# Experts computed for chosen token-expert pairs in 23 static tiles, with the routing moved into self-attention

## Chip, cores and metric

One core of a Trainium2 chip (trn2). The time is the device time of one launch in microseconds; of the kernel before three runs were taken (1611.67, 1611.69 and 1613.4, median 1611.69). Profiles are of one execution.

## What is computed

Sixteen sequences of 64 tokens (1024 rows of 512 numbers) pass one layer: cross-attention over 1601 context rows each, causal self-attention, and a mixture of experts. All in float32. The last part, which the change is about:

```python
scores = jnp.einsum('bsd,ed->bse', x, w_gate_router)          # 8 experts
topk_scores, topk_idx = jax.lax.top_k(scores, 2)
topk_probs = jax.nn.softmax(topk_scores, axis=-1)
weights = jnp.sum(topk_probs[..., None] * jax.nn.one_hot(topk_idx, E), axis=-2)
gate = jnp.einsum('bsd,efd->bsef', x, w_gate_proj)             # f = 192
up = jnp.einsum('bsd,efd->bsef', x, w_up_proj)
out = jnp.einsum('bsef,edf,bse->bsd', silu(gate) * up, w_down_proj, weights)
```

Here x is the layer-normalised input, and the result is added to the input. Of the 1024 x 8 (token, expert) pairs, 2048 have a weight that is not zero.

## The kernel before, in words

Everything is written by hand: each engine has its own instruction list in a block per stage, and they meet at semaphores. The stages are prepare, cross_attention (to about 1190 us), self_attention (L1303, to 1371) and experts (L1716). A block ends when all engines are through.

**Precision.** Where a product is made of two float32r halves, split_product (L93) issues three matmuls for each block of 128 rows of the contraction: high by high, high by low, low by high. The halves come from a copy with a cast to float32r (high) and a subtraction (low). transposes (L78) turns blocks of 128x128 by a matmul with the identity.

**self_attention.** Four rounds of two chunks of 128 tokens (i = 0..3, u = 0, 1), three of them in a loop on each engine, each with: queries, keys and values (L1603, L89), scores (L1628), softmax on VectorE (L1503 to L1510), exp on ScalarE (L1415), transposed probabilities, the weighted sum (L1654), normalisation, the transposed output, the output product (L89); between these stand the pieces of the next round's cross-attention output product (L1582) and its normalisation (L1466 to L1487). stats2 (L1536) takes statistics of the finished x. Beside it SP loads the weights of the first two experts into expert_raw in three transfers, and POOL computes their high and low halves (L1371, L1373).

**experts.** First the routing for all 8 chunks of 128 tokens: normalise (L1839), transpose, copy to moe_xT (L1799), split (L1801, L1843), product with the router's 8 columns (L89, eight matmuls of 128x8 a chunk in float32), then on VectorE scores, the two largest, their indices, softmax of two and one row of 8 weights per token (L1860 to L1877). After that a loop over four pairs of experts, two of them in its body, with 8 chunks each. A chunk has gate and up for both experts of the pair, 384 columns each (24 matmuls), silu on ScalarE (L1811), the product with up and the weight on VectorE (L1892), three transposes, the halves (L1816, L1901), the down product of 512 columns (9 matmuls) and the addition into x_sb (L1906). TensorE's order is gate_up(t), transposes of t-1, down2(t-2). Beside it SP loads the next pair's weights, VectorE casts their high halves (L1883, 128x1536 each) and POOL subtracts for the low ones (L1785). At the end SP stores the 8 chunks of x (L1776).

## Time and profile before

| | us |
|---|---|
| median of 3 runs | 1611.69 |
| the profiled execution's own time | 1612.94 |
| its span, first to last instruction | 1611.1 |
| TensorE busy (matmul) | 1535.0, 95% of the span |
| weight loads of TensorE | 1299.7, 81% |
| VectorE busy | 848.6, 53% |
| ScalarE busy | 741.3, 46% |
| POOL busy | 464.7, 29% |
| cross-attention ends | about 1190 |
| self-attention ends | about 1371 |
| first matmul of the experts (L100) | 1394.1 |
| last matmul of the experts | 1607.6 |

How to read it: L100 is the line of the matmul in split_product, whoever calls it; the tiles tell the stage. Matmuls overlap in the pipeline, so one of 384 columns is shown with 335 ns while the next starts 172 ns later; weight loads (PEld) have their own row. Idle time is put before an instruction in brackets, with what ended it. The DMA share is of 16 engines.

### The profile page before, as it was taken

The page shows a single profiled execution, that of the slowest core. Times are in us where ns is not written, and L with a number is a line of the kernel's source. Part 1 is how long each engine was busy: PE and PEld are TensorE (multiplying, and loading weights), DVE is VectorE, ACT ScalarE, POOL GpSimd, SP SyncE. Part 2 cuts the span into 40 slices and gives each one's busy share as a digit, 9 for nine tenths or more (in the row PEclk, how much of TensorE's full clock was granted, in tenths as well). Part 3 has the DMA queues.
Part 4 walks back from the last instruction along what each step waited for, and adds up shares of the span by engine and source line. Part 5 has one row for each costly group of instructions (what it writes and reads, how often), then busy time and mean ns, then how long its engine had stood idle before and what let it go on. Part 6 is the DMA issues. An engine that isn't in the chain of part 4 may idle for free. (4 is left out here: it accounts for less than half of the span.)

```text
span 1611.1 us, 41874 instructions
## 1 busy us (share of the span) xinstructions
PE 1535.0 (95%) x16226; PEld 1299.7 (81%) x16226; DVE 848.6 (53%) x1793; ACT 741.3 (46%) x1515; POOL 464.7 (29%) x492
## 2 busy tenths in 40 slices
PE   5789999999999999999999999999977998899999
PEld 2378888888888888888888888888856666899998
DVE  6756555555655555555565555556535554433333
ACT  2246555555655555555555555555532232311111
POOL 3233333333333333333333333333330000022102
PEclk9989999999999999999999999999998999699999
DMA  6030011000110100001000110000020000121011
GB/s 233 17 94 26 21 29 32 18 25 28 32 28 15 32 28 28 18 29 28 28 20 27 28 32 15 28 28 16 3 60 1 0 0 1 60 59 60 20 38 52
DMA packets 35920, 53.81 MB, mean 33 GB/s; under 512 B 7091, under 2 KB 15670, under 8 KB 35766
## 3 DMA queue, kind: packets, MB, share of 16 engines
q1 hardware_dynamic: 35332, 51.44, 10.5%
q8 instruction: 126, 2.06, 0.5%
q14 instruction: 28, 0.23, 0.0%
q10 hardware_dynamic: 434, 0.08, 0.0%
HBM read 48.89 MB, written 2.62 MB: 32 GB/s over the span
## 5 line engine op out<-in xcount | busy, mean ns | idle before, releaser
L1044 POOL TENSOR_TENSOR ksq<-kc 128x512 f32<-128x512 f32 x200 | 208.1, 1041 | 431.7 <-DVE kc L1089 429.8
L1089 DVE TENSOR_TENSOR kc<-psum,bk_sb 128x512 f32<-128x512 f32 x200 | 138.2, 691 | 239.7 <-PE psum L100 239.6
L954 ACT COPY v_sb<-psum 128x512 f32<-128x512 f32 x192 | 112.7, 587 | 282.3 <-PE psum L100 282.3
L968 ACT ACTIVATE probs<-psum 128x1024 f32<-128x1024 f32 x208 | 202.8, 1023 | 81.7 <-PE psum L1211 81.6
L1211 PE MATMUL psum<-qbd,k 64*128 64x128 f32 x3328 | 216.0, 279 | 4.4 <-issue 4.4
L1037 POOL TENSOR_TENSOR y_lo<-y_sb,y_hi 128x256 fp32r<-128x256 f32 x190 | 139.3, 733 | 231.5 <-ACT y_hi L927 231.4
L1211 PEld LDWEIGHTS psum<-qbd,k 64*128 64x128 f32 x3328 | 195.0, 188 | 11.2 <-issue 7.2
L1228 PEld LDWEIGHTS psum<-v_sb,probs 128*64 128x64 f32 x6144 | 186.9, 138 | 17.6 <-issue 17.5
L1228 PE MATMUL psum<-v_sb,probs 128*64 128x33 f32 x6144 | 197.6, 224 | 0.0
L1095 DVE TENSOR_REDUCE kss<-ksq 128x16 f32<-128x512 f32 x200 | 136.4, 682 | 111.3 <-POOL ksq L1044 111.3
L100 PE MATMUL psum<-wk_hi,y_hi 128*128 128x512 f32 x400 | 176.8, 442 | 11.1 <-issue 9.0
L100 PE MATMUL psum<-wv_hi,y_hi 128*128 128x512 f32 x400 | 158.8, 397 | 0.2 <-ACT v_sb L954 0.2
L100 PE MATMUL psum<-wk_hi,y_lo 128*128 128x512 f32 x400 | 158.0, 395 | 0.0
L100 PE MATMUL psum<-wk_lo,y_hi 128*128 128x512 f32 x400 | 157.4, 393 | 0.0
L100 PE MATMUL psum<-wv_hi,y_lo 128*128 128x512 f32 x400 | 157.3, 393 | 0.0
L100 PE MATMUL psum<-wv_lo,y_hi 128*128 128x512 f32 x400 | 157.2, 393 | 0.0
L940 ACT ACTIVATE k<-psum,cols_sb 128x512 f32<-128x512 f32 x192 | 150.6, 785 | 9.2 <-PE psum L81 8.7
L1104 DVE SCALAR_TENSOR_TENSOR kn<-kc,kr 128x512 f32<-128x512 f32 x200 | 141.4, 707 | 7.3 <-DVE kr L117 0.4
L81 PEld LDWEIGHTS psum<-ident_sb,kn 128*128 128x128 f32 x800 | 99.3, 140 | 27.8 <-issue 1.7
L81 PE MATMUL psum<-ident_sb,kn 128*128 128x128 f32 x800 | 120.1, 273 | 1.3 <-ACT k L940 1.3
L115 DVE SCALAR_TENSOR_TENSOR ktmp<-ktmp,kseed 128x16 f32<-128x16 f32 x200 | 116.5, 583 | 6.8
L1785 POOL TENSOR_TENSOR wg_lo<-expert_raw,wg_hi 128x1536 fp32r<-128x1536 f32 x4 | 14.0, 3490 | 309.6 <-DVE wg_hi L1883 309.6
(223 smaller groups left out, 2311.1 us busy)
## 6 DMA issues: line engine op xcount, KB each, us to landing
y_sb<-in_y SPq DMA_DIRECT2D x48, 512.0 KB, 3.7
expert_raw<-in_wg SPq DMA_DIRECT2D x5, 768.0 KB, 5.1
expert_raw<-in_wu SPq DMA_DIRECT2D x5, 768.0 KB, 4.6
expert_raw<-in_wd SPq DMA_DIRECT2D x5, 768.0 KB, 4.6
out_dram<-x_sb SPq DMA_DIRECT2D x8, 256.0 KB, 2.0
x_sb<-in_x SPq DMA_DIRECT2D x1, 1536.0 KB, 10.2
wq<-in_wq SPq DMA_DIRECT2D x4, 256.0 KB, 5.1
xa_wo<-in_wo SPq DMA_DIRECT2D x1, 1024.0 KB, 12.2
```

The costliest lines, as they stand in the source:

```text
L81: last = pe.transpose(bank[:, k * P:(k + 1) * P], src[:, k * P:(k + 1) * P], ident)
L100: last = pe.matmul(bank, lhs, rhs, start=(n == 0), stop=(n == len(todo) - 1))
L115: nc.vector.scalar_tensor_tensor(out=tmp, in0=tmp, scalar=-0.5, in1=seed, op0=ALU.mult, op1=ALU.mult).then_inc(second, 1)
L940: last = nc.scalar.activation(k32[:, buf(n)], bank, ACT.Identity, scale=g.cols[:, 2:3], bias=g.cols[:, 3:4])
L968: nc.scalar.activation(probs[:, buf(u), :], psum[:, bank:bank + 2, :].rearrange("p a n -> p (a n)"), ACT.Exp, scale=SCALE).then_inc(s["ex" ...
L1037: nc.gpsimd.tensor_tensor(g.y_lo[:, buf(n)], src, g.y_hi[:, buf(n)].bitcast(F32), ALU.subtract).then_inc(s["ylo"], 1)
L1044: nc.gpsimd.tensor_tensor(sq[:, buf(n)], kc[:, buf(n)], kc[:, buf(n)], ALU.mult).then_inc(s["ksq"], 1)
L1089: nc.vector.tensor_tensor(kc[:, buf(n)], psum[:, K_BANK, :], g.bk[:], ALU.add).then_inc(s["kb"], 1)
L1095: nc.vector.tensor_reduce(ss[:, buf(n)], head_view(sq[:, buf(n)]), AX_X, ALU.add).then_inc(s["krd"], 1)
L1104: nc.vector.scalar_tensor_tensor(out=head_view(kn[:, buf(n)]), in0=head_view(kc[:, buf(n)]), scalar=HD ** 0.5, in1=spread(kr[:, buf(n)], H ...
L1211: last = pe.matmul(out[n][a], k32[rows, k_buf(u), n, :], g.qbd[rows, n, :], start=not guarded, stop=True, skip_group_check=True)
L1228: last = pe.matmul(psum[j * SQ:(j + 1) * SQ, V_BANK if n else O_BANK, p * VW1:(p + 1) * VW1], probs[:, buf(u), place(h) * SQ:(place(h) + 1 ...
```

## The change

**Layout.** A row of x in SBUF grows from 512 to 520 numbers: behind the 512 stand the token's number (TOK), the number plus 2048 (TOK_S), the difference of its two weights (GAIN), the smaller weight (WEIGHT), the first expert (FIRST), the higher expert's number (HIGH), 1/sigma (RSTD) and -mean/sigma (SHIFT). A DRAM tensor "slots" has a region of 1024 such rows for each expert and a ninth one. Blank rows, with token numbers in a spare part of the output, are written over all of it in cross_attention: nine DRAM-to-DRAM writes of 1024 rows (2.1 MB each) on SP's queue. The output tensor grows to 3712 rows, of which the first 1024 count.

**Routing.** Rounds i-1 = 0..2 are routed within self_attention's round i, and round 3 in the experts' block. TensorE transposes x as it is (not normalised), multiplies by the router's columns (the mean's part is subtracted by the column sums, route_columns), and counts for each token how many before it chose the same expert (route_ranks: four matmuls of up to 16 columns with a triangular and a ones matrix). VectorE takes statistics, logits, the two largest, indices, weights and each row's place; nearly every step waits for the one before (link: a semaphore per instruction). POOL then writes the 128 rows of each chunk to two places in slots: four indirect DMAs of 128 rows a round. self_attention's loop is unrolled. POOL no longer splits weights there; SP loads two experts' weights (1 MB each) in place of one pair's.

**Tables.** After the last round VectorE computes from the counts for each of 23 tiles its expert, its first row in slots, and where its weights lie (27 small operations). 23 = 16 + 7 is the most that 2048 pairs can fill with tiles of 128 rows of one expert; the number of tiles is the same whatever the routing.

**Tiles.** For each tile SP loads 128 rows (5 buffers), ScalarE normalises them, TensorE transposes them (4), ScalarE and VectorE make halves, TensorE multiplies with gate and up of one expert (12 matmuls of 384 columns, 192 for gate and 192 for up), silu of 192 columns, VectorE's product in three pieces, two transposes, halves, down (6 matmuls of 512), ScalarE multiplies by the weight. POOL stores the rows of y at the token's row of the output where this expert is the token's lower one, adds the layer's input rows to y, and adds the sum by an accumulating indirect DMA where it is the higher one; the other case of each goes to spare rows. A store waits until the store of the tile before has landed. All weights, high and low, stay in SBUF; experts 0 and 1 and the third block of the down weights are split before the first tile, experts 2 to 7 after tiles 0, 1, 2, 4, 5 and 6 (AFTER), the high half on ScalarE, the low one on VectorE, 2048 columns each. TensorE reads three numbers per tile into registers (steer) and addresses its weights by them.

The diff, cut to its core (lines taken out are those of the old experts and of the splits in self_attention):

```diff
+                def blanks(e, n):
+                    sp.dma_start(io["slots"][bass.ds(e * REGION, n * 2 * P), :].rearrange("(a p) c -> a p c", a=n),
+                                 io["blank"][bass.ds(e, 1)].to_broadcast([n, 2 * P, ROW])).then_inc(s["blank"], 16)
+                blanks(E_, E_ // 2)
...
+                    blanks(i, REGION // P // 2)
...
+def route_scatter(nc, io, g, pool, i):
+    r = g.route
+    pool.wait_ge(r.s["place"], i + 1)
+    for u in range(2):
+        for n in range(PICK):
+            nc.gpsimd.indirect_dma_start(
+                io["slots"][:, :], bass.IndirectOffsetOnAxis(ap=r.target[:, i, n, u:u + 1], axis=0),
+                g.x[:, i * 2 + u, :], None).then_inc(r.s["slots"], 16)
...
+    for u in range(2):
+        last = nc.vector.max_index(out=r.idx[:, i, u, :], in_max=r.top[:, i, u, :], in_values=r.logits[:, i, u, :])
+    r.link(dve, nc.vector.tensor_tensor(r.gap[:, i], r.top[:, i, :, 1], r.top[:, i, :, 0], ALU.subtract))
+    nc.vector.tensor_tensor(r.gap_n[:, i], r.gap[:, i], g.x[:, i * 2:i * 2 + 2, RSTD], ALU.mult).then_inc(r.s["gap"], 1)
+    r.link(dve, nc.vector.tensor_copy(r.chosen[:, i], r.idx[:, i, :, 0:PICK]))
+    for n in range(PICK):
...
                 def steps(i, more):
                     qkv(i, 0)
+                    if i:
+                        pe.wait_ge(s["x2"], done(i - 1, 1))
+                        pe.wait_ge(s["xe"], done(i, 1))
+                        route_turn(g, pe, i - 1, 0, psum[:, TR, :])
                     qkv(i, 1)
+                    if i:
+                        pe.wait_ge(r.s["xe"], i * 2 - 1)
+                        route_turn(g, pe, i - 1, 1, psum[:, TR, :])
                     scores(i, 0)
+                    if i:
+                        route_product(g, pe, psum, i - 1, 0)
+                        route_product(g, pe, psum, i - 1, 1)
                     if more:
                         out_product(i + 1, 0, 0)
                     scores(i, 1)
                     if more:
...
+                def rows_in(j):
+                    first = table(sp, "first", j, 0, SLOT_ROWS - P)
+                    if j >= XB:
+                        sp.wait_ge(s["total"], j - XB + 1)
+                    sp.dma_start(rows[:, j % XB, :], io["slots"][bass.ds(first, P), :]).then_inc(s[f"rows{j % XB}"], 16)
+                sp.wait_ge(s["low0"], 1)
+                sp.dma_start(raws[0].rearrange("p (n d) -> p n d", d=D), io["wd_rest"]).then_inc(s["raw0"], 16)
+                sp.wait_ge(s["tables"], 1)
+                sp.wait_ge(r.s["slots"], 16 * ROUNDS * 2 * PICK)
+                for j in range(XB):
+                    rows_in(j)
+                for e in range(2, 5):
+                    load(e)
+                for j in range(XB, TILES):
+                    rows_in(j)
+                    if j in LOADS:
+                        load(LOADS[j])
+                for n in range(2):
+                    sp.wait_ge(s[f"first{n}"], 16 * ((TILES + 1 - n) // 2))
+                    sp.wait_ge(s[f"second{n}"], 16 * ((TILES + 1 - n) // 2))
...
+            @blk.gpsimd
+                pool.wait_ge(s["whi"], 1)
+                nc.gpsimd.tensor_tensor(block(0, 1), raws[0], block(0, 0).bitcast(F32), ALU.subtract).then_inc(s["low0"], 1)
+                route_scatter(nc, io, g, pool, last)
+                for j in range(TILES):
+                    n = j % 2
+                    pool.wait_ge(s["y"], j + 1)
+                    if j:
+                        pool.wait_ge(s[f"first{1 - n}"], 16 * ((j + 1) // 2))
+                    nc.gpsimd.indirect_dma_start(
+                        io["out"][:, :], bass.IndirectOffsetOnAxis(ap=at_first[:, j:j + 1], axis=0),
+                        y[:, n, :], None).then_inc(s[f"first{n}"], 16)
+                    if j >= 2:
+                        pool.wait_ge(s[f"second{n}"], 16 * (j // 2))
+                    nc.gpsimd.tensor_tensor(total[n], y[:, n, :], rows[:, j % XB, 0:D], ALU.add).then_inc(s["total"], 1)
+                    pool.wait_ge(s["total"], j + 1)
+                    nc.gpsimd.indirect_dma_start(
+                        io["out"][:, :], bass.IndirectOffsetOnAxis(ap=at_second[:, j:j + 1], axis=0),
+                        total[n], None, compute_op=ALU.add).then_inc(s[f"second{n}"], 16)
...
+                def x_norm(j):
+                    act.wait_ge(s[f"rows{j % XB}"], 16 * (j // XB + 1))
+                    if j >= 2:
+                        act.wait_ge(s["tr"], j - 1)
+                    row = rows[:, j % XB, :]
+                    nc.scalar.activation(xn[:, j % 2], row[:, 0:D], ACT.Identity, bias=row[:, SHIFT:SHIFT + 1],
+                                         scale=row[:, RSTD:RSTD + 1]).then_inc(s["xn"], 1)
...
+                def scale(j):
+                    act.wait_ge(s["dn"], j + 1)
+                    act.wait_ge(s["weight"], j + 1)
+                    if j >= 2:
+                        act.wait_ge(s[f"first{j % 2}"], 16 * (j // 2))
+                        act.wait_ge(s["total"], j - 1)
+                    nc.scalar.activation(y[:, j % 2], psum[:, DN + j % 2, :], ACT.Identity, scale=weight[:, j:j + 1]).then_inc(s["y"], 1)
...
+                route_evac(nc, g, act, last, 0, psum[:, TR, :])
+                route_evac(nc, g, act, last, 1, psum[:, TR + 1, :])
+                route_seed(nc, g, act, last)
+                high(0)
+                route_exp(nc, g, act, last)
+                high(1)
+                act.wait_ge(s["raw0"], 16)
+                nc.scalar.copy(rest[:, 0].rearrange("p n d -> p (n d)"), raws[0]).then_inc(s["rest_hi"], 1)
+                x_norm(0)
+                x_norm(1)
+                x_high(0)
+                x_high(1)
+                for j in range(TILES + 1):
+                    if 0 < j and j + 1 < TILES:
+                        x_high(j + 1)
+                    if j < TILES:
+                        silu(j)
+                    if j:
+                        scale(j - 1)
+                    if j < TILES:
+                        h_high(j)
+                    if j + 2 < TILES:
+                        x_norm(j + 2)
+                    for e in range(2, E_):
+                        if AFTER[e] == j:
+                            high(e)
...
+                route_stats(nc, g, last, 1)
+                route_norm(nc, g, dve, last)
+                route_logits(nc, g, dve, psum, last)
+                route_top(nc, g, dve, last)
+                route_rows(nc, g, dve, last)
+                route_place(nc, g, dve, psum, last)
+                route_tables(nc, g, dve)
+                dve.sem_inc(s["tables"], 1)
+                dve.wait_ge(s["low0"], 1)
+                low(1)
+                dve.wait_ge(s["rest_hi"], 1)
+                nc.vector.tensor_tensor(rest[:, 1].rearrange("p n d -> p (n d)"), raws[0],
+                                        rest[:, 0].rearrange("p n d -> p (n d)").bitcast(F32), ALU.subtract).then_inc(s["rest_lo"], 1)
+                x_low(0)
+                x_low(1)
+                for j in range(TILES):
+                    weights(j)
+                    hidden(j)
+                    if 0 < j and j + 1 < TILES:
+                        x_low(j + 1)
+                    h_low(j)
+                    for e in range(2, E_):
+                        if AFTER[e] == j:
+                            low(e)
...
+                def gate_up(j, base, need):
+                    pe.wait_ge(s["xhi"], j + 1)
+                    pe.wait_ge(s["xlo"], j + 1)
+                    pe.wait_ge(s["wlo"], need)
+                    if j >= 2:
+                        pe.wait_ge(s["hid"], j - 1)
+                    terms = [(x_hi[:, j % 2, k, :], x_lo[:, j % 2, k, :], w[:, bass.ds(base + k * 2 * F, 2 * F)],
+                              w[:, bass.ds(base + (WHALF + k * 2 * F), 2 * F)]) for k in range(KD)]
+                    split_product(pe, psum[:, GU + j % 2, 0:2 * F], terms).then_inc(s["gu"], 1)
...
+                def steer(j):
+                    return (table(pe, "block", j, 0, (E_ - 1) * WBLOCK), table(pe, "at", j, 0, (E_ // 2 - 1) * D),
+                            table(pe, "need", j, 1, E_))
...
+                held = [steer(0)]
+                turn(0)
+                for j in range(TILES + 1):
+                    if j + 1 < TILES:
+                        held.append(steer(j + 1))
+                        turn(j + 1)
+                    if j < TILES:
+                        gate_up(j, held[j][0], held[j][2])
+                    if j:
+                        down(j - 1, held[j - 1][0], held[j - 1][1])
+                    if j < TILES:
+                        turn_hidden(j)
...
```

## Rows read from the trace of the kernel before

**Rows 1.** The page, part 2: the clock granted to TensorE, in 40 slices of 40.3 us, in tenths.

```profile
PEclk9989999999999999999999999999998999699999
```

**Rows 2.** Busy time by stretch (us, count), then PEclk, DMA share, GB/s.

```profile
1217.60:1371.00 153.40, 141.25 (x1067) 102.19 (x1065) 75.85 (x152) 45.32 (x104) 0.00 (x0) 0.99 0.00 1
1371.00:1394.10 23.10, 19.96 (x96) 19.69 (x96) 10.42 (x27) 11.32 (x19) 0.00 (x0) 0.51 0.32 104
1394.10:1398.50 4.40, 4.40 (x15) 4.40 (x15) 3.52 (x33) 1.49 (x2) 0.00 (x0) 0.50 0.00 0
1398.50:1609.00 210.50, 209.49 (x1140) 194.87 (x1139) 71.96 (x143) 28.05 (x64) 41.84 (x12) 1.00 0.14 43
...
1347.00:1362.00 15.00, 9.53 (x121) 7.12 (x122) 9.32 (x14) 5.70 (x11) 0.00 (x0) 1.00 0.00 1
```

**Rows 3.** Timeline (start, us) of one chunk's weight loads in the expert stage.

```profile
1402.51 0.19 PEld L100 LDWEIGHTS psum<-wu_hi,moe_xhi 128*128 128x128 f32 x1
...
1404.59 0.42 PEld L81 LDWEIGHTS psum<-ident_sb,moe_h 128*128 128x128 f32 x3
...
1404.99 0.19 PEld L100 LDWEIGHTS psum<-wg_hi,moe_xhi 128*128 128x128 f32 x1
...
1409.48 0.19 PEld L100 LDWEIGHTS psum<-wd_hi,moe_hhi 128*128 128x128 f32 x1
...
1411.46 0.19 PEld L100 LDWEIGHTS psum<-wg_hi,moe_xhi 128*128 128x128 f32 x1
```

**Rows 4.** Timeline and page: single durations (page: xcount, busy, mean ns, idle).

```profile
L1044 POOL TENSOR_TENSOR ksq<-kc 128x512 f32<-128x512 f32 x200 | 208.1, 1041 | 431.7 <-DVE kc L1089 429.8
...
L940 ACT ACTIVATE k<-psum,cols_sb 128x512 f32<-128x512 f32 x192 | 150.6, 785 | 9.2 <-PE psum L81 8.7
...
1331.12 0.38 ACT L1396 COPY sa_xT<-psum 128x256 f32<-128x256 f32 x1
...
1350.17 1.22 DVE L1508 TENSOR_REDUCE sa_mx<-sa_s 128x16 f32<-128x1024 f32 x1
```

**Rows 5.** Timeline of DVE, POOL and PE at the head of self-attention (start, us).

```profile
1200.30 2.30 DVE L1469 TENSOR_TENSOR x_sb<-x_sb,t 128x512 f32<-128x512 f32 x1
...
1204.42 3.01 DVE L113 SCALAR_TENSOR_TENSOR sa_rtmp<-sa_mv,sa_rseed 128x1 f32<-128x1 f32 x1 [0.60 <-ACT sa_rseed L108]
...
1209.07 3.54 DVE L1487 TENSOR_SCALAR sa_xn<-x_sb,sa_mv,sa_rs 128x512 f32<-128x512 f32 x1
...
1213.24 0.69 DVE L1469 TENSOR_TENSOR x_sb<-x_sb,t 128x512 f32<-128x512 f32 x1
...
1204.00 3.42 POOL L1373 TENSOR_TENSOR wu_lo<-expert_raw,wu_hi 128x1536 fp32r<-128x1536 f32 x1
...
1212.66 1.11 PE L81 MATMUL psum<-ident_sb,sa_xn 128*128 128x128 f32 x4 [8.58 <-DVE sa_xn L1487]
```

**Rows 6.** Timeline at the end of self-attention and in the routing.

```profile
1369.51 1.28 DVE L1536 BATCH_NORM_STATS2 x_stats<-x_sb 128x6 f32<-128x512 f32 x2
...
1378.45 1.83 PEld L89 LDWEIGHTS psum<-wr,moe_xT 128*128 128x128 f32 x8
...
1397.41 0.20 DVE L1871 RECIPROCAL moe_w<-moe_ex 128x8 f32<-128x8 f32 x1
1397.65 0.17 DVE L1872 TENSOR_TENSOR moe_w<-moe_ex,moe_w 128x8 f32<-128x8 f32 x1
```

**Rows 7.** DMA: the page's issues (count, KB, us to landing) and SP's timeline.

```profile
y_sb<-in_y SPq DMA_DIRECT2D x48, 512.0 KB, 3.7
...
out_dram<-x_sb SPq DMA_DIRECT2D x8, 256.0 KB, 2.0
...
y_tail<-in_y_tail SPq DMA_DIRECT2D x8, 128.0 KB, 2.9
...
409.23 0.60 SPq L853 DMA_DIRECT2D v_last<-vd_dram  x1
...
433.07 46.02 SPq L135 DMA_DIRECT2D y_sb<-in_y  x3
```

More of the change, by code:

```diff
@@ new lines, in route_turn, with route_columns, route_product @@
+def route_turn(g, pe, i, u, bank):
+    transposes(pe, bank, g.x[:, i * 2 + u, 0:D], g.ident[:]).then_inc(g.route.s["tr"], 1)
+def route_columns(g, pe, psum):
+    r = g.route
+    pe.wait_ge(r.s["ones"], 1)
+    pe.wait_ge(r.s["wr"], 16)
+    for k in range(KD):
+        last = pe.matmul(psum[:, ROUTE, LOGITS:LOGITS + E_], r.ones[:], r.wr[:, k, :], start=(k == 0), stop=(k == KD - 1))
+    last.then_inc(r.s["columns"], 1)
+def route_product(g, pe, psum, i, u):
+    r = g.route
+    pe.wait_ge(r.s["xe"], i * 2 + u + 1)
+    if u == 0:
+        if i == 0:
+            pe.wait_ge(r.s["sums"], 1)
+        else:
+            pe.wait_ge(r.s["place"], i)
+    product(pe, psum[:, ROUTE, LOGITS + u * E_:LOGITS + (u + 1) * E_], r.xT[:, u], r.wr[:]).then_inc(r.s["rp"], 1)
@@ L1342, in rounds @@
         def rounds(eng, steps):
-            with eng.Fori(0, NT // 2 - 1) as i:
-                steps(i, True)
-            steps(NT // 2 - 1, False)
+            for i in range(NT // 2):
+                steps(i, i + 1 < NT // 2)
         def last_one(i, u):
@@ new lines, in experts, with block, raw_turn, table @@
+        at_second = sb("moe_at_second", [P, TILES], U32)
+        t = r.tables
+        def block(e, part):
+            at = e * WBLOCK + part * WHALF
+            return w[:, at:at + WHALF]
+        ORDER = (0, 1, 1, 0, 1, 0, 1, 0)
+        AFTER = (0, 0, 0, 1, 2, 4, 5, 6)
+        LOADS = {5: 5, 6: 6, 8: 7}
+        last = ROUNDS - 1
+        def raw_turn(e):
+            return 1 + sum(ORDER[n] == ORDER[e] for n in range(2, e)) + (ORDER[e] == 0)
+        def table(eng, name, j, low, top):
+            return eng.value_load(t[name][0:1, j:j + 1], min_val=low, max_val=top)
```

642 lines of the change are left out of this document (380 added, 262 removed).

## The prediction

> **What bounds the kernel now.** I read the stretches first. From about 84 us on TensorE is nearly always busy at the granted clock of 1.0 [rows 1]. Self-attention (1217.6 to 1371) has it busy 141 of 153 us; the routing (1371 to 1394) 20 of 23 us at a clock of 0.51; the expert pairs 209.5 of 210.5 us at 1.00, with VectorE a third and ScalarE an eighth busy [rows 2]. So each matmul taken from the expert stage counts in full, until another engine or a chain of waits takes over. Then I read the pace of one chunk: 12 split matmuls of 384 columns take 2.08 us, three transposes 0.40 us, nine of 512 columns 1.98 us [rows 3]. A chunk has 24, 3 and 9 of them: 6.6 us; 32 chunks make the 211 us. All 8 experts are computed for all 1024 tokens though two are chosen.
>
> **What the change does to that sum.** 32 chunks of two experts become 23 tiles of one. A tile's TensorE work is 4 + 2 transposes (0.54 + 0.27), 12 matmuls of 384 (2.08) and 6 of 512 (1.32), 4.2 us; 23 of them are 97 us against 211. That is not the new time. The new body has an order that ScalarE closes: in its turn j it does the next x_high, silu(j), scale(j-1), h_high(j) and only then x_norm(j+2), and TensorE starts its next turn with the transposes of that x_norm. From the end of down(j-1) to those transposes: semaphore 0.2, scale 0.79 and x_norm 0.79 (like the activation with column operands), h_high 0.38 (128x256 copy) [rows 4], less 0.1 of overlap at each of two hand-overs, 0.1 for the last semaphore: 2.0 us. TensorE has only turn_hidden in it (0.27), so a turn is 2.0 + 0.54 + 2.08 + 1.32 = 5.95; I take **6.1 us**, for waits not seen here.
>
> Other loops per tile. VectorE: x_low 0.69 (as the addition in [rows 5]), five small and three medium operations about 1.3, h_low 0.45: 2.4 us, inside. POOL: store, addition, adding DMA. The addition is a little over the 1.04 us of a 128x512 product [rows 4], 1.2. An indirect DMA issued by POOL stands nowhere in this trace. Its nearest rows are an issue on SP, 0.59 us [rows 7], and POOL's dearest instruction, 3.42 us [rows 5]; I take 1.1, by POOL's own 1.04 us over the same 128 rows. POOL is then busy 3.4 of 6.1 us. Rows of slots: five buffers; row tile j is asked for when the addition j-4 is done, at down(j-4) + 0.2 + 0.8 + 1.1 + 1.2 = 3.3, and lands 3.2 us later (128 KB take 2.9, 512 KB 3.7 [rows 7]), at 6.5; x_norm(j) wants it at 6.1 + 1.1 = 7.2. It is in time by 0.7 us: this is what is late next. TensorE's three register loads per tile have no row; from below they cost nothing, from above they fill the 1.7 us in which TensorE waits for x_norm, and that cover is why I cost them at nothing. If they took 1 us each, a turn would be about 7.
>
> **Splits beside the first tiles.** The halves of experts 2 to 7 are split after tiles 0, 1, 2, 4, 5, 6: 2048 columns, ScalarE about 1.9 us, VectorE 2.3 us (twice the 1.22 us of 1024 [rows 4]). high(e) fits in ScalarE's idle time, low(e) then sits in front of the next hidden(j), which I work out at 1.5 us late: 6 x 1.5 = 9, and 1 for the last load, which is asked for late: **+10 us**. The first gate_up starts after idle time; now the first 4.4 us of matmuls run at 0.50 [rows 2], twice as long as at 1.00: +2.
>
> Loop: tile 0 to its hidden transposes 5, gate_up(1) and down(0) 4, 21 turns of 6.1 = 128, last down 3.2; 140, with splits and clock **152 us** from the first gate_up to the last down.
>
> **Routing.** Rounds 0 to 2 go into self-attention. TensorE gets per round 8 transposes (0.135 each), 8 products of 8 columns (8 take 1.83 at half clock [rows 6], so 0.11 each at full) and 4 rank matmuls: 2.5 us, three times, and 0.5 for the column sums: +8.0. VectorE gets some 5 us a round, in places where it waits for TensorE; I add 1 for what isn't covered (0 to 6). Against it, POOL's splits of the first experts leave self-attention. They hold VectorE up now: an addition takes 2.30 us where the same takes 0.69 later, an operation on 128x1 3.01 until POOL's wu_lo is done (1204.00 + 3.42), xn 3.54, and TensorE waits 8.58 us for that chain [rows 5]. That wait goes nearly whole: -8.2. Net +1. One bn_stats pair no longer ends the stage (1.28 us [rows 6]): -1.2. The expert block begins at 1370.9.
>
> The last round then runs alone. Transposes, evacuation, seed: 2.6; refinement and logits to 3.9. ScalarE splits expert 0 until 4.5, and POOL computes its low half, 3.42 x 2048/1536 = 4.6 us, until 9.3. The routing's subtraction of two SBUF operands falls into that, and by [rows 5] waits for its end. From 9.3: a dependent small operation starts 0.24 us after the last [rows 6], take 0.22; picks, ranks and places reach 12.6. Four scatters of 1.1 on POOL, landed at 19.4; the tables (27 operations, 5.5 us) are done beside them. Then the first row load 3.7 with its register load, x_norm 0.8, transposes at half clock 1.3, x_high 0.6, x_low 0.7: first gate_up at 26.5, so **1397.4** where it is 1394.1 now.
>
> **Tail.** Scale 1.0, store 1.1, addition 1.2, adding issue 1.1, landing 3.2: 7.6 us where it is now 0.7 for the addition and 2.0 for the store [rows 7].
>
> **Blanks.** Nine writes of 2.1 MB go between the loads of cross-attention. From the slope of [rows 7], 0.8 us per 384 KB, one takes about 7 us. After v_last at 409.23 the next y load is issued 23.8 us later [rows 7], so I cost it at nothing. The Trainium skill, page DMA: Bandwidth & Descriptors, section on why a DMA increments by 16, says that a DMA whose slowest dimension is 4 uses at most 4 of the 16 engines; by that it is about 20 us, still under 23.8. No row here shows it.
>
> **Sum.** 1397.4 + 152 + 7.6 = 1557 of span, against 1611.1. The profiled execution took 1612.94, the median of the runs is 1611.69, 0.6 above its span. I predict **1558 us**, 3.3% less.
>
> **Rivals.**
> - The turn is shorter, 5.2 us: x_norm and scale cost 0.6, and the splits fall into ScalarE's and VectorE's idle time. 1558 - 21 - 6 = about 1530. For it: VectorE is idle more than half. Against: the order on ScalarE is in the code. 0.12.
> - The rows come late, or the register loads don't hide: turn 7 to 7.8. 1558 + 23 x 0.9 to 1.7 = 1579 to 1597. For it: only 0.7 us of slack, three transfers of 256 KB and the weights on the same DMA engines. 0.24.
> - **Slower:** POOL becomes the bound through its two indirect DMAs. Its turn is 2a + 1.3 with a for one; with a = 1.1 it isn't seen, from a = 2.4 it rules, and the gain of 54 us is gone at a turn of 8.4, a = 3.6. At a = 4.2 the turn is 9.7 and the time 1558 + 83 + 20 for scatter and tail = 1660. For it: no row bounds a except POOL's 3.42 us. Against: POOL's ordinary instructions on 128 rows are at 1 us. 0.11.
> - **Slower, by the clock.** TensorE waits 1.7 us each turn. It ran at 1.00 from 1347 to 1362 while 9.5 of 15 us busy, with such gaps, and at 0.51 with 8-column products while 20 of 23 us busy [rows 2]. A tile turn is 4.2 of 6.1 busy with wide matmuls, nearer to the first. At the lower level (1.2 GHz) the 3.9 us behind x_norm double: turn 10, 1558 + 90 = 1648. The Trainium skill, TensorE: Matmul & The Clock Gate, Part 1, says that the throttled state is the default and activity releases it; by that rule each long wait is a risk, and the time would be this 1648. 0.05.
> - It doesn't do what it says: more tiles are computed than the tokens need (23 are static, whatever the counts), but no fewer; dense work can't stay, as the pair tiles are gone. Some other loss eats all: within 0.2%, 0.03.
>
> **How the numbers follow.** The forecast's own case, 1540 to 1578, has 0.45. With the two neighbours it reaches 1527 to 1606, which holds 0.8: what is left out is the two slower cases and the ends. A measurement of this kernel tells 0.2% (3.2 us) from no change. Faster by more: 0.45 + 0.12 + 0.24 = 0.81; same 0.03; slower 0.16.
>
> **What would show it.** In the profile after: TensorE waiting about 1.6 us for xn before each tile's transposes, ScalarE's x_norm the releaser; tiles 6.1 us apart, 7.6 after those with a split; granted clock 1.00 in the loop; the first gate_up near 1397; a VectorE subtraction of some 4 us beside POOL's low half; no 8.58 us wait at 1212. Wrong if x_norm waits for rows, if POOL is busy or in issues most of a turn, if the first gate_up is after 1405, or if y_hi waits in cross-attention.

## The result, and the profile after

The kernel after the change takes **1575.39 us**, median of four runs (1572.8 to 1577.6), beside 1611.7 for the kernel before in the same job: a ratio of 0.9773 (95% interval 0.9761 to 0.9785), 2.3% less. The profiled execution took 1574.65 us with a span of 1572.7. The forecast was 1558, so the direction and the range held, and of the forecast gain of 54 us 36 came. The 15.7 us between the forecast span of 1557 and 1572.7 lie in three places: the loop over the tiles (161.8 us for 152), the tail (12.0 for 7.6) and the start of the first product (1398.87 for 1397.4).

Stretches of the kernel after, answering to [rows 2]: self-attention, last routing, the tiles beside which weights are split, the other tiles, the end. Columns are busy time (count) of PE, PEld, DVE, ACT, POOL, then PEclk, DMA share, GB/s.

```profile
1218.00:1371.50 153.50, 145.49 (x1123) 106.07 (x1121) 86.28 (x247) 48.95 (x116) 11.74 (x12) 1.00 0.06 22
1371.50:1398.90 27.40, 7.61 (x41) 6.71 (x41) 18.24 (x60) 10.63 (x12) 8.37 (x5) 0.55 0.40 125
1398.90:1458.50 59.60, 41.64 (x184) 36.64 (x182) 33.20 (x85) 29.83 (x45) 25.25 (x18) 0.83 0.66 186
1458.50:1553.00 94.50, 69.99 (x336) 62.39 (x336) 56.35 (x140) 35.17 (x69) 53.89 (x42) 0.89 0.51 110
1553.00:1572.70 19.70, 6.11 (x29) 4.42 (x27) 4.11 (x11) 3.02 (x6) 11.54 (x9) 0.82 0.50 92
```

TensorE is now busy 72% of the expert loop, where it was busy all of it, and the granted clock, 1.00 in that stage before, is 0.83 and 0.89. Four turns one after the other, cut at the starts of x_norm, in the same columns:

```profile
1458.44:1464.35 5.91, 4.38 (x24) 3.79 (x24) 4.06 (x10) 2.58 (x7) 3.86 (x3) 1.00 0.47 108
1464.35:1472.14 7.79, 5.90 (x24) 5.32 (x24) 4.05 (x10) 2.57 (x6) 3.85 (x3) 0.78 0.59 122
1472.14:1478.05 5.91, 4.38 (x24) 3.79 (x24) 4.05 (x10) 2.58 (x7) 3.86 (x3) 1.00 0.48 108
1478.05:1485.99 7.94, 5.89 (x24) 5.34 (x24) 4.04 (x10) 2.57 (x6) 3.84 (x3) 0.79 0.58 123
```

The first and third are the turn of the prediction within 0.04 us (5.95 was its sum, before the rounding up to 6.1). In the others the same 24 matmuls take 5.9 us instead of 4.4. The timeline of TensorE over two of these waits (start, us, then the idle time before):

```profile
1459.32 0.66 PE L88 MATMUL psum<-ident_sb,x_sb 128*128 128x128 f32 x4 [1.53 <-ACT x_sb L2131]
...
1465.59 0.63 PE L88 MATMUL psum<-ident_sb,x_sb 128*128 128x128 f32 x4 [1.90 <-ACT x_sb L2131]
...
1467.27 0.52 PE L107 MATMUL psum<-experts,moe_xlo 128*128 x1
```

x_norm began at 1464.35 and takes 0.82: it was done at 1465.17, and the transposes began 0.42 us later. In the fast turn they followed it at once. The last row shows the low clock: the same product takes 0.34 us in the fast turns, and the granted clock from 1467 to 1469 is 0.50. Over the 13 turns from 1458.44 to 1547.88, six of them slow, the mean is 6.88 us.

### The profile page after: what moved, and what is told of

It reads as the page before. It is cut to its first block and busy times, and to the rows that moved or that the text cites. A ratio compares the mean times of both kernels' runs of the same rounds, so it can differ in the third digit from the quotient of the medians.

```text
span 1572.7 us, 41557 instructions
## 1 busy us (share of the span) xinstructions
PE 1437.7 (91%) x15666; PEld 1199.6 (76%) x15666; DVE 877.3 (56%) x1984; ACT 783.5 (50%) x1575; POOL 519.4 (33%) x561
## 5 line engine op out<-in xcount | busy, mean ns | idle before, releaser
L1227 PEld LDWEIGHTS psum<-qbd,k 64*128 64x128 f32 x3328 | 195.0, 188 | 11.5 <-issue 7.2
L107 PEld LDWEIGHTS psum<-wk_hi,y_hi 128*128 128x128 f32 x400 | 75.5, 189 | 29.6 <-issue 10.9
```

The source lines that it names most:

```text
L107: last = pe.matmul(bank, lhs, rhs, start=(n == 0), stop=(n == len(todo) - 1))
L1227: last = pe.matmul(out[n][a], k32[rows, k_buf(u), n, :], g.qbd[rows, n, :], start=not guarded, stop=True, skip_group_check=True)
```

## Experiments

Theories at the start. **A:** the long turns are the clock's, which falls when TensorE waits too long ahead of the transposes. **B:** something else recurs every other turn (rows, register loads, a split) and the clock only follows. And on what makes the wait: ScalarE's chain, or TensorE's own three register loads, which the prediction had costed at nothing. In the profiles of all thirteen versions with the change, the last addition of cross-attention starts between 1191.4 and 1197.0, though nothing in that part differs but e8's blanks; so beside the times I compare the loop alone, from the first product of the experts to the end of the last.

**e1: TensorE's wait filled.**

```diff
                     if j < TILES:
                         turn_hidden(j)
+                    if j + 2 < TILES:
+                        for n in range(6):
+                            pe.matmul(psum[:, GU + (j + 1) % 2, 0:P], r.before, r.before, start=True, stop=True)
```

> Six 128x128 products of two constant tables are put on TensorE behind the transposes of each tile's hidden layer, in the place where TensorE waits (1.5 us ahead of the fast turns, 1.9 to 2.06 us ahead of the slow ones), so that it is busy there; what they write is read by nobody. If the slow turns of 7.8 us are slow because the clock falls to 0.78 after the wait (my theory): the clock stays at 1.00 all through the loop, every turn behind the weight splits is 5.9 to 6.1 us, and the program takes 1555 to 1562 us. If they are slow by something else that recurs every other turn (rows that come late, register loads, the DMAs of the splits) and the low clock only follows from the waiting: the turns keep alternating between 5.9 and 7.8 us, and the time stays within 2 us of 1575. If the added products delay the transposes, the turns are all 6.1 us plus that delay.

Measured: 1565.45 us (1563.4 to 1567.8), though each turn got more work. Behind the splits:

```profile
1464.00:1542.00 78.00, 69.20 (x440) 62.83 (x438) 49.88 (x122) 31.94 (x63) 47.49 (x38) 1.00 0.57 120
```

The clock is 1.00 and no turn there is 7.8 us; A holds, though the time is 3 us above the range expected. But the turns are 5.98 to 6.59 us (mean 6.36), not 5.9 to 6.1, so something beside ScalarE's chain delays the transposes: at 1484.51 they start 0.66 us behind the end of x_norm.

**e2: no register loads.**

```diff
-                    return (table(pe, "block", j, 0, (E_ - 1) * WBLOCK), table(pe, "at", j, 0, (E_ // 2 - 1) * D),
-                            table(pe, "need", j, 1, E_))
+                    e = j // 3
+                    return (e * WBLOCK, e % (E_ // 2) * D, e + 1)
```

> TensorE takes each tile's weights by constants (expert j div 3) and not by numbers that it loads from the tables: this leaves out the choice of the expert by the tables on TensorE, so that the tiles get other experts' weights; the rows, the stores and all other steps stay. If TensorE's register loads and the addresses worked out from them cost time at a turn (stretches of 0.57 to 0.74 us in which it waits for nothing, in some turns): turns get 0.5 us shorter, 1560 to 1566 us. If they are hidden by the wait for ScalarE's x_norm: within 2 us of 1575. Under the theory that the clock makes the slow turns they stay.

Measured: 1557.56 us (1556.2 to 1558.1), 17.8 less than after: more than either expectation allowed. From 1454.9 on all 13 turns are 5.90 to 5.91 us, TensorE waits 1.53 us in each but the first (1.17) and the clock is 1.00. The slow turns were the clock's, but what lowered it came with the loads. That a load is hidden by the wait for x_norm was true only of the first 1.5 us.

**e3 and e4: x_norm earlier on ScalarE.** In e3 it stands ahead of h_high, in e4 ahead of both scale and h_high (shown):

```diff
+                    if j + 2 < TILES:
+                        x_norm(j + 2)
                     if j:
                         scale(j - 1)
                     if j < TILES:
                         h_high(j)
-                    if j + 2 < TILES:
-                        x_norm(j + 2)
```

> ScalarE makes the normalised rows of tile j+2 ahead of the high part of the hidden layer of tile j, instead of behind it. The chain from the end of down(j-1) to the transposes of tile j+2 loses one operation of 0.38 us. By my sum (turn = chain on ScalarE 2.0 + products and transposes 3.9) the turn is 5.5 us at the full clock, 22 turns give 9 us, and if the shorter wait also keeps the clock up in more turns, up to 20 us more: 1550 to 1567 us. If the turn is bound by something other than that chain (the rows' arrival, GpSimd's period, a clock that alternates whatever the wait is): within 3 us of 1575.

> ScalarE makes the normalised rows of tile j+2 right behind the silu of tile j, ahead of the scaling of tile j-1's result and of the high part of tile j. They then no longer wait for down(j-1), and the transposes of tile j+2 follow without a wait. By my sum the turn is then bound by TensorE's own work of 4.0 to 4.3 us or by GpSimd's period of 4.46 us (two indirect DMAs 0.98 and 1.58, addition 1.30, gaps), so 4.5 to 4.9 us, at the full clock: 1527 to 1545 us. If the wait for ScalarE is only replaced by one for rows or for GpSimd's additions, turns stay near 5.9 to 6.9: 1560 to 1575 us.

Measured: 1575.13 us (1572.7 to 1578.6) and 1572.63 us (1572.4 to 1573.9). Both expectations of a shorter turn fell. The timeline of e4 says why:

```profile
1481.55 0.81 ACT L2131 ACTIVATE x_sb<-x_sb 128x512 f32<-128x512 f32 x1
...
1482.52 0.38 PE L88 MATMUL psum<-ident_sb,moe_h 128*128 128x128 f32 x2
...
1484.45 0.63 PE L88 MATMUL psum<-ident_sb,x_sb 128*128 128x128 f32 x4 [1.55 <-issue]
...
1487.45 0.81 ACT L2131 ACTIVATE x_sb<-x_sb 128x512 f32<-128x512 f32 x1
...
1490.69 0.63 PE L88 MATMUL psum<-ident_sb,x_sb 128*128 128x128 f32 x4 [1.89 <-issue]
```

x_norm ends at 1482.36, and the transposes that need it start at 1484.45, after 1.55 us in which TensorE waits for nothing shown, and 1.89 us in the next turn. What stands there in its queue are the three loads. So two things of nearly one length end at the same place: 1.53 us of ScalarE's chain, and three loads of 1.5 to 2.3 us together (2.7 once). Taking ScalarE's away shows the loads.

**e5: one load instead of three, the wait for the splits by a constant.**

```diff
-                    return (table(pe, "block", j, 0, (E_ - 1) * WBLOCK), table(pe, "at", j, 0, (E_ // 2 - 1) * D),
-                            table(pe, "need", j, 1, E_))
+                    base = table(pe, "block", j, 0, (E_ - 1) * WBLOCK)
+                    at = pe.snap((base & ((E_ // 2 - 1) * WBLOCK)) >> 3, min_val=0, max_val=(E_ // 2 - 1) * D)
+                    return base, at, min(j + 1, E_)
```

> TensorE loads one number for each tile instead of three: the address of the expert's block. The place in the other weight table is worked out from it in a register, and the wait for the weight splits is by the constant min(j+1, 8). All results stay as they are. If the three loads in a row (about 0.5 us each by my reading: 1.55 to 1.89 us of idle TensorE ahead of the transposes though x_norm was long done) are what made the waits of 1.9 to 2.06 us, and these in turn the low clock: the idle time ahead of the transposes is 1.53 us in every turn, set by ScalarE, the clock stays at 1.00, turns are 5.9 us, and the time is that of the kernel with constant weights, 1556 to 1560 us. If the gain with constant weights came from the other order of experts or from addresses without registers in the matmuls: 1570 to 1576 us.

Measured: 1573.15 us (1572.8 to 1576.7), by the letter the number of the rival; but the trace shows both. Behind the splits all 13 turns are 5.90 to 6.00 us at 1.00, as expected, and ahead of them three turns take 12.92, 11.57 and 12.53:

```profile
1442.02 1.00 PE L107 MATMUL psum<-experts,moe_xhi 128*128 x2 [4.07 <-DVE experts L2233]
...
1454.70 1.00 PE L107 MATMUL psum<-experts,moe_xhi 128*128 x2 [3.83 <-DVE experts L2233]
...
1466.31 1.00 PE L107 MATMUL psum<-experts,moe_xhi 128*128 x2 [3.86 <-DVE experts L2233]
```

My own edit made these. The constant lets tiles 5, 6 and 7 (counted from 0) wait for the splits of the sixth, seventh and eighth expert, which stand in the lists of ScalarE and VectorE only behind tiles 4, 5 and 6 (for tile 5 the cast starts at 1437.14 and the subtraction ends at 1441.67); by the tables these tiles need no such wait (e9). Behind them the turns are as short as with constants (e2), although the addresses still come from a register, so constant addresses weren't what made e2 fast.

**e6 and e7: e5 with x_norm behind the silu, and with the addition on VectorE.**

```diff
-                    nc.gpsimd.tensor_tensor(total[n], y[:, n, :], rows[:, j % XB, 0:D], ALU.add).then_inc(s["total"], 1)
...
+                    nc.vector.scalar_tensor_tensor(out=total[n], in0=psum[:, DN + n, :], scalar=weight[:, j:j + 1],
+                                                   in1=rows[:, j % XB, 0:D], op0=ALU.mult, op1=ALU.add).then_inc(s["total"], 1)
```

(These pieces are e7's; VectorE does the addition for tile j-1 behind h_low(j), and down(j) waits for that of tile j-2.)

> The one load of the run before, and x_norm of tile j+2 right behind the silu of tile j. Each alone leaves the other as the bound; if these two are the two near-equal waits ahead of the transposes, both together take the wait down to some 0.5 to 0.7 us, and the turn to 4.9 us (3.9 to 4.3 of TensorE's own work and the rest of the wait), with GpSimd's period of 4.46 us as the next bound: 22 turns of 1.0 us less than 5.9, so 1532 to 1542 us. If VectorE (1.96 us of blocked weight operation beside GpSimd's addition in each turn) or GpSimd binds first: turns of 5.4 us and more, 1545 to 1556 us.

> As the run before, and the addition of the two terms made by VectorE straight from PSUM (result times weight plus the stored row) instead of by GpSimd from ScalarE's copy: GpSimd keeps only its two indirect DMAs (0.98 and 1.58 us a turn), and VectorE's first weight operation no longer runs beside a GpSimd addition. If that addition blocks VectorE (1.96 us for a 128x1 operation): the operation takes 0.2 us; VectorE gets 0.7 us of addition for it; GpSimd's period falls from 4.46 to about 3 us. The tail behind the last down gets 1.3 us shorter or more. Time: 3 to 12 us less than the run before if GpSimd or VectorE was the bound there, 1 to 3 us less if TensorE was. If VectorE's addition from PSUM delays the hidden layer's low part: not faster than the run before.

Measured: e6 1554.81 us (1553.5 to 1556.3), e7 1548.09 us (1547.3 to 1550.4). With both covers gone the turns behind the splits are 4.6 to 4.8 us at 1.00, with a few longer ones (one pair in e6 of 5.98 and 3.89). e6 misses its 1532 to 1542 by the same three late splits (10.3, 11.4 and 12.2 us). e7's VectorE and GpSimd:

```profile
1503.35 0.42 DVE L2227 TENSOR_TENSOR moe_hlo<-psum,moe_hhi 128x256 fp32r<-128x256 f32 x1 [0.75 <-ACT moe_hhi L2149]
1503.69 0.74 DVE L2240 SCALAR_TENSOR_TENSOR x_sb<-psum,moe_weight,x_sb 128x512 f32<-128x512 f32 x1
1504.35 0.21 DVE L2200 SCALAR_TENSOR_TENSOR moe_second<-x_sb,route_table_expert 128x1 f32<-128x1 f32 x1
...
1504.88 0.98 POOL L2108 DMA_INDIRECT out_dram<-route_y,moe_at_first  x1 [1.84 <-DVE x_sb L2240]
```

The same 128x1 operation took 1.97 us in the kernel after, ending with GpSimd's addition (first two rows of the tail, below). The fused operation costs 0.74 us, the blocked one fell by 1.76. The 6.7 us less than e6 are partly the tail: 10.2 us for 13.8 between the last product and the end.

**e8: blanks with 256 rows outermost.**

```diff
-.rearrange("(a p) c -> a p c", a=n),
-                                 io["blank"][bass.ds(e, 1)].to_broadcast([n, 2 * P, ROW])).then_inc(s["blank"], 16)
+.rearrange("(a p) c -> p a c", a=n),
+                                 io["blank"][bass.ds(e, 1)].rearrange("a p c -> p a c").to_broadcast([2 * P, n, ROW])).then_inc(s["blank"], 16)
```

> The blank rows are written with the dimension of 256 rows outermost in the access pattern instead of the one of 4 copies; same contents, same bytes. If the old form is served by few DMA engines and holds up what is queued behind it (y_tail landing 21.5 us instead of 2.9, v_last 15.4 instead of 3.6), the landing times go back below 6 us, the cross-attention ends 1 to 2 us earlier and the time is 1573 to 1574.5 us. If it was the bytes and not their form: landing times stay, and the time is 1575 to 1577 us.

Measured: 1575.03 us (1570.6 to 1576.5): no difference that these runs can tell. The page's issues, after and then e8 (KB each, median us to landing); before, y_tail took 2.9 [rows 7]:

```profile
y_tail<-in_y_tail SPq DMA_DIRECT2D x8, 128.0 KB, 21.5
...
v_last<-vd_dram SPq DMA_DIRECT2D x16, 32.0 KB, 15.4
```

```profile
slots_dram<-in_blank SPq DMA_DIRECT2D x9, 2080.0 KB, 10.8
...
y_tail<-in_y_tail SPq DMA_DIRECT2D x8, 128.0 KB, 9.4
...
v_last<-vd_dram SPq DMA_DIRECT2D x16, 32.0 KB, 8.1
```

The form of the write matters to what is queued behind it, more than two to one. The landing below 6 us that I expected didn't come. What the form does to cross-attention stands at the end of the next section.

**e9: one load, the wait worked out from it.**

```diff
-                    return base, at, min(j + 1, E_)
+                    return base, at, (min(j + 1, 2) if j < 2 else pe.snap((base >> 12) + 1, min_val=1, max_val=E_))
```

> The one load of before again, but the wait for the weight splits is worked out in a register from the same number (address / 4096 + 1), so that tiles 6 to 8 no longer wait for splits of experts that they don't use. The order on ScalarE is that of the kernel after the change. In the run with the constant, three turns took 11.6 to 12.9 us, with TensorE waiting 3.8 to 4.1 us for the split each time, and all turns behind them 5.9 us at clock 1.00. If the three loads made the slow turns: those turns stay at 5.9 us, the three long ones become 6 to 7.5, so 17 us less than 1573: 1554 to 1559 us, the time of the kernel with constant weights. If the even turns came from the long waits before them: 1570 to 1576 us, turns alternating again.

Measured: 1562.92 us (1558.9 to 1564.1), 12.5 less than after; the time is 4 us above the range expected, the turns are as expected, 6.90, 7.48 and 6.92 for the three long ones and then turns like this one:

```profile
1475.71:1481.66 5.95, 4.42 (x24) 3.80 (x24) 4.07 (x10) 2.58 (x6) 3.87 (x3) 1.00 0.62 137
```

This changes nothing but where three numbers come from. The loop takes 145.9 us instead of 161.8. These 16 us are more than the 9.8 by which the loop missed its forecast. Of them 3.6 don't show in the profile's end, since its first product comes later, at 1402.5 for 1398.9 of after; that is decided before the expert block.

**e10: e9 with e4's order and e7's addition.** The diffs are those above.

> One load with the wait from the register, x_norm behind the silu, the addition on VectorE. In the run with the constant wait the turns behind the weight splits were 4.6 to 5.0 us and three turns 10.7 to 11.1 us. If those three fall to 5.5 to 6.5 us: 14 to 17 us less than 1548, so 1530 to 1535 us. If the weights' arrival (loads of 1 MB asked one after the other) binds the first nine turns in any case, now that the turns are shorter than in the kernel before: 1540 to 1546 us, with waits of TensorE for VectorE's splits left.

Measured: **1535.52 us** (1533.4 to 1541.7), ratio 0.9519 to the kernel before (0.9503 to 0.9535): 4.8% less instead of 2.3%. The loop takes 125.5 us. The time is half a us above the range expected. Of the three long turns of e7 (11.1, 10.7 and 11.1 us) two are now 4.7 us and one 8.3; in all, four of the eight turns beside the splits still take 6.7 to 8.3 us, with TensorE waiting 1.6 to 2.0 us for VectorE ahead of the hidden transposes.

```profile
1463.50:1515.90 52.40, 49.40 (x266) 42.06 (x265) 32.06 (x121) 28.30 (x56) 27.99 (x23) 1.00 0.77 166
```

Eleven turns of 4.76 us, TensorE 94% busy: it is the bound again.

**e11: the first expert's low half on VectorE.** The subtraction goes from GpSimd's list to VectorE's, behind the tables; the load of the other weight table goes behind the second row load, and its splits behind x_high(1) and x_low(1).

```diff
-                pool.wait_ge(s["whi"], 1)
-                nc.gpsimd.tensor_tensor(block(0, 1), raws[0], block(0, 0).bitcast(F32), ALU.subtract).then_inc(s["low0"], 1)
...
+                dve.wait_ge(s["whi"], 1)
+                nc.vector.tensor_tensor(block(0, 1), raws[0], block(0, 0).bitcast(F32), ALU.subtract).then_inc(s["low0"], 1)
```

> As the run before, and the low part of the first expert's weights is made by VectorE behind its tables (2.3 us) instead of by GpSimd ahead of the scatters (4.5 us); the load and the splits of the other weight table follow behind the first rows. If GpSimd's subtraction is what makes VectorE's small routing operation take 3.56 us: that operation takes 0.2 to 0.3 us, and the tables and the first product come 3 us earlier (first product at 1395.5 to 1396 instead of 1398.9), the time 2 to 3.5 us less than the run before. If the later split of the other table holds the first down up: within 1 us of the run before, with TensorE waiting for it ahead of the first down.

Measured: 1535.25 us (1534.2 to 1537.7), no difference to e10. The mechanism is there, first as it is after the change, then in e11:

```profile
1376.08 4.49 POOL L2100 TENSOR_TENSOR experts<-expert_raw,experts 128x2048 fp32r<-128x2048 f32 x1 [6.63 <-ACT experts L2124]
...
1377.03 3.56 DVE L1499 TENSOR_TENSOR route_gap<-route_top 128x2 f32<-128x2 f32 x1
```

```profile
1381.37 0.14 DVE L1499 TENSOR_TENSOR route_gap<-route_top 128x2 f32<-128x2 f32 x1
```

From the cast of expert 0 to the first product it is 21.2 us, where e10 has 24.6. In the profiles those 3.4 us are there; between the medians they are not. The profiled run of e10 is its slowest (1541.69 us), that of e11 too (1537.72), and they do differ by 4 us; with the spread of e10's runs, 8 us, I can't say what the medians hide. The later split of the other table isn't what took them back: the loop takes 125.0 us, for 125.5 in e10.

**e12: e11 with four split turns filled.**

```diff
+                    if j in (0, 2, 5, 7):
+                        for n in range(6):
+                            pe.matmul(psum[:, GU + (j + 1) % 2, 0:P], r.before, r.before, start=True, stop=True)
                     if j < TILES:
                         turn_hidden(j)
```

> The run before with six 128x128 products that nobody reads put on TensorE ahead of the transposes of the hidden layers of tiles 0, 2, 5 and 7, where it waited 1.4 to 1.8 us for VectorE behind a weight split and where the clock then showed 0.75 to 0.81 over the turn (6.9, 7.8, 8.0 and 8.2 us, against 4.7 to 4.8 of the turns between). If the clock is what makes more than the wait itself of these turns: they fall to 6.2 to 6.6 us (4.7 and the wait of 1.5 to 1.9), together 5 to 7 us: 1528 to 1531 us. If the turns are long because VectorE's split delays several steps one after the other: they stay, and the time is within 2 us of 1535. If the waits fall at other tiles once these are filled: in between, with the low clock moved to those.

Measured: 1533.75 us (1531.5 to 1537.6), ratio 0.9517 (0.9503 to 0.9531); not told apart from e11 (0.952). The four filled turns (x_norm of tiles 2, 4, 7 and 9) take 5.81, 5.49, 6.25 and 6.23 us, all at 1.00, where e11 had 6.86, 7.82, 8.03 and 8.21 at 0.75 to 0.81. In exchange two that had been 4.77 and 5.10 us are 7.81 and 8.36 at 0.78 and 0.80, and another takes 6.18. Over the eight turns it is 51.3 us against 50.3. The waits come at other tiles once some are filled, the third case of the expectation.

## Why the prediction came out as it did

**The turn's sum was right, its cover was not.** "TensorE's three register loads per tile have no row ... that cover is why I cost them at nothing": this is the step that failed. The other end stood beside it, a turn of about 7 at 1 us a load. Measured behind the splits, the loads take 1.5 to 2.3 us together, some 0.5 to 0.8 each (with one load and the early x_norm, e7, TensorE waits 0.24 to 0.50 us), so no more than 0.8 us of them stand out behind the 1.53 us of ScalarE's chain. That would be 6.2 or 6.3 us a turn (e8 has a few of them: 6.2 and 6.3 us at 1.00). (Beside the splits they are longer: two turns of after wait 2.81 and 2.40 us for nothing shown.) The mean of 6.88 comes from the second step of the same fault: "granted clock 1.00 in the loop". Six of the 13 turns were granted 0.78 or 0.79, which adds 1.5 us to their products. By e9 against after, loads and clock together cost 16 us of loop and 12.5 of time; filling the wait alone (e1), which brings back the clock and leaves the loads, gives 11.5 us of loop. That 1575 lay inside the range says little for the path: the low clock came in through a cover that failed by a few tenths.

**The clock rival had the right place and the wrong size.** It said that each wait of 1.7 us puts the clock at risk, and priced all turns at the lower level: 1648. The Trainium skill's page TensorE: Matmul & The Clock Gate, Part 1, holds the throttled state to be the default that activity releases; the trace agrees in the direction (waits filled in e1, clock at 1.00 behind the first two turns), but about half of the turns were hit, each for some 3 us, and behind the splits none where the wait was 1.53 (e2, e9).

**Late rows: right to be rejected, by wrong working.** The prediction gave them 0.7 us of slack and rested 0.24 on this rival together with the loads. Five buffers mean that row tile j is asked for when the addition of tile j-5 is done, not j-4; the slack is a turn longer, and no x_norm in the loop waited for rows. The rival's range of 1579 to 1597 was just missed by 1575, and its half about the loads was the true one.

**GpSimd.** Taken as 1.1 each, the indirect DMAs cost 0.98 (store, scatter 0.96) and 1.58 us (adding): period 4.46 instead of 3.4 us, still inside a turn of 5.9. The slower rival needed 2.4. It mattered where nothing covers it, in the **tail**, timeline of ScalarE and GpSimd:

```profile
1554.41 1.97 DVE L2201 SCALAR_TENSOR_TENSOR moe_second<-x_sb,route_table_expert 128x1 f32<-128x1 f32 x1
1555.05 1.30 POOL L2113 TENSOR_TENSOR x_sb<-route_y,x_sb 128x512 f32<-128x512 f32 x1
...
1560.73 0.69 ACT L2158 ACTIVATE route_y<-psum,moe_weight 128x512 f32<-128x512 f32 x1 [2.36 <-PE psum L107]
1561.09 1.58 POOL L2115 DMA_INDIRECT out_dram<-moe_total,moe_at_second  x1 [0.28 <-POOL moe_total L2113]
1562.98 0.97 POOL L2108 DMA_INDIRECT out_dram<-route_y,moe_at_first  x1 [0.31 <-issue]
1563.98 1.27 POOL L2113 TENSOR_TENSOR x_sb<-route_y,x_sb 128x512 f32<-128x512 f32 x1
1565.53 1.58 POOL L2115 DMA_INDIRECT out_dram<-x_sb,moe_at_second  x1 [0.28 <-POOL x_sb L2113]
```

From the last product's end at 1560.7: 2.3 us to the store, since GpSimd was still with tile 21 (1.0 was predicted), store 1.0 (1.1), addition and hand-over 1.55 (1.2), adding issue 1.6 (1.1), and 5.6 from its end to the end of the span (3.2). All but the store were taken too small, the landing of an adding DMA by most: it was priced like a plain load. The first two rows are the pair that e7 took apart.

**The splits** were predicted at 10 us. The eight turns from x_norm(1) to x_norm(9) took 61.8 us where the sum gives 8 x 6.1 + 10 = 58.8, or 60.8 with the 2 us for the low clock of the first products, which fall in the first of these turns. Here too the clock is in what was measured: e9 needs 57.5.

**Routing and self-attention.** The expert block starts at 1372.0 (1370.9), and from there it is 26.9 us to the first product (26.5); VectorE's small operation waits for GpSimd's subtraction as [rows 5] said, 3.56 us. The chain of blocked operations at the head of self-attention is gone: where [rows 5] has 2.30, 3.01 and 3.54, now

```profile
1202.50 0.69 DVE L1735 TENSOR_TENSOR x_sb<-x_sb,t 128x512 f32<-128x512 f32 x1
...
1205.02 0.16 DVE L120 SCALAR_TENSOR_TENSOR sa_rtmp<-sa_mv,sa_rseed 128x1 f32<-128x1 f32 x1 [0.60 <-ACT sa_rseed L115]
...
1205.60 0.55 DVE L1753 TENSOR_SCALAR sa_xn<-x_sb,sa_mv,sa_rs 128x512 f32<-128x512 f32 x1
```

**Blanks at nothing:** the last addition of cross-attention starts at 1190.46 before and between 1191.4 and 1197.0 in the thirteen profiles behind the change, and the prediction had nothing for it. The stage takes a reciprocal once per sequence, sixteen times (RECIPROCAL rinv<-o_sb), and the distance from before at each of these shows three parts. At the first, near 173 us, the profiles lie from 2.0 us early to 2.4 late; the cause wasn't looked into. From there to the fourteenth all thirteen, e8 too, slip by 1.4 to 1.7 us, evenly. Between the fourteenth and the fifteenth the twelve with the old form lose another 1.0 to 4.2 us, and e8 loses 0.1. There ScalarE waits for nothing that the profile shows, and in the twelve TensorE then waits 0.7 to 2.3 us for it. In five of them (e1, e5, e7, e9, e10; waits of 1.9 to 2.3) the granted clock falls behind this one wait, to 0.91 over the 20 us from 1110, and these lose 3.8 to 4.2 us; the other seven, at 1.00, lose 1.0 to 2.1. ScalarE's wait before, in after and in e8:

```profile
1103.33 0.78 ACT L940 ACTIVATE k<-psum,cols_sb 128x512 f32<-128x512 f32 x1 [0.45 <-issue]
```

```profile
1106.57 0.78 ACT L956 ACTIVATE k<-psum,cols_sb 128x512 f32<-128x512 f32 x1 [4.02 <-issue]
```

```profile
1105.55 0.78 ACT L956 ACTIVATE k<-psum,cols_sb 128x512 f32<-128x512 f32 x1 [1.87 <-issue]
```

It falls into the time of the ninth blank write, issued at 1094.21 in after. Two microseconds of that write, in after and in e8 (the last two numbers are the DMA share and GB/s):

```profile
1101.00:1103.00 2.00, 2.00 (x13) 1.65 (x12) 1.90 (x5) 0.59 (x1) 1.18 (x2) 1.00 0.25 106
```

```profile
1101.00:1103.00 2.00, 2.00 (x11) 1.57 (x11) 1.28 (x4) 0.86 (x4) 1.27 (x2) 1.00 1.06 378
```

The page DMA: Bandwidth & Descriptors of the Trainium skill, in its section on why a DMA increments by 16, lets the slowest dimension set the number of engines, at most 4 for a dimension of 4; the trace agrees, with a share of 0.25 of 16 engines. At 106 GB/s the 2.1 MB take 20 us, as the prediction worked out by that rule, and not the 7 us that it costed. The hole of 23.8 us did cover the next y load; ScalarE's wait is what it didn't have. What ScalarE waits for isn't shown, e8 has one profile, of its fastest run (1570.6, where its others reach 1576.5), and whether the even slip comes from the blanks isn't settled: a kernel without blanks wasn't tried.

## What to carry to other kernels

Where two things wait in one hole, cost both, and state the shorter cover's margin: here 1.53 us of one engine's chain lay over loads of 1.5 to 2.3 us; a shorter chain alone gave 0 to 3 us (e3, e4), fewer loads alone 12.5 (e9), and both, with the addition moved, 40 (e10). A number loaded into a register of the engine that sets the pace costs something like half a microsecond (three together 1.5 to 2.3 us; with one, where x_norm is done early, TensorE's wait is 0.24 to 0.65 us in e6 and e7); load one and work the others out. A wait that is made simpler must not ask for more than the old one did (e5: 10 us more than e9).

## What was not expected of the hardware

- Three register loads on TensorE in a row: 1.54 to 2.3 us behind the splits of e4, differing from turn to turn in the same program. Behind a turn at the low clock they are mostly short: TensorE's wait there is 1.53 to 1.70 us after all six slow turns behind the splits of after, and 1.54 to 1.58 after five of e4's six slow turns. This is how long waits and slow turns come to alternate; why the loads are shorter there wasn't looked into.
- Behind the splits of after the granted clock fell to 0.50 for some 3 us in six of the seven turns with waits of 1.86 to 2.23 us, and in none of those with 1.53 us there, in e2 or in e9. The length of one wait doesn't decide it alone: e4 has three turns in a row of 6.38 us with waits of 2.00 to 2.04 at 1.00, and e8 five in a row at 1.00 with waits of 1.85, 2.27, 1.77, 2.25 and 1.95. What decides was not found.
- An adding indirect DMA holds GpSimd 1.58 us where a storing one takes 0.98, and lands after 4.9 us (median).
- A VectorE operation on one number a partition with two SBUF inputs took 1.97 us beside GpSimd's 1.30 us addition, and 0.21 with the addition gone.
